# Causal attention: maxima subtracted beside full-array work, row tiles of two batches adjacent, h normalised a step ahead, weights halved on ScalarE

## The chip, the cores and the metric

The program runs on one core of a Trainium2 chip. The metric is device time in microseconds (us), from the start of one execution to its end. The engines of the core work from queues of their own and wait for each other on semaphores: PE (TensorE, matrix multiplication; PEld is its weight load), DVE (VectorE), ACT (ScalarE), POOL (GpSimd) and SP (SyncE, which issues transfers here).

## The reference

The network is a decoder of two layers on x of shape 16 x 128 x 256, each with self attention, cross attention and a gated MLP. Only the first self attention is touched by the change:

```python
x = x + _L0_attn_ref(_layernorm(x, axis=-1), L0_attn_Wqkv, L0_attn_Wout)

def _L0_attn_ref(x, Wqkv, Wout):          # 16 heads of 16, S = 128
    qkv = x @ Wqkv.T                      # split into q, k, v by head
    q = q * cos + rotate_half(q) * sin
    k = k * cos + rotate_half(k) * sin
    scores = jnp.einsum('bhqd,bhkd->bhqk', q, k) * scale
    scores = jnp.where(causal[None, None], -jnp.inf, scores)
    attn = jax.nn.softmax(scores, axis=-1)
    out = jnp.einsum('bhqk,bhkd->bhqd', attn, v)
    return out @ Wout.T
```

The cross attention that follows reads weights that are split into a high and a low half, so that products of fp32r halves add up to the product in fp32. The split is made during the first self attention, one sixteenth in each of its steps.

## The kernel before

The six sublayers run one after the other, each as a block of five programs, one for an engine. The first is `causal_attention`. It takes the 16 batches one at a time (128 tokens are the 128 partitions, 256 features the columns) through a software pipeline that is written out by hand: `batches` calls `step(t, s)` for t from -2 to 17 on each engine, and in step t an engine works on batches t - 2 to t + 2. The order of an engine's work is the order in which its `step` names it; nothing reorders it later.

Heads are worked on in four slots of four. Slot g uses rows 32g to 32g + 31 of TensorE's array, so that scores are made by row tiles (32 x 128 of the array). A batch has two pairs of slots, pair 0 (slots 0 and 1) and pair 1 (slots 2 and 3), and goes this way:

- DVE normalises x into `h` (`dve_normalise`, L144). PE turns h (`turn`, L670), ACT copies it out as hT, PE projects queries and keys (`project_queries_and_keys`, L691). DVE multiplies by the rotary tables (`multiply_by_tables`, L530 and L533) and adds (`add_turned`, L541). PE turns the result (L670 with `weights_even` as its source). ACT copies it out for bf16 (`narrow_queries_and_own_keys`, L452 and L454) and for fp32 (`copy_keys_and_own_queries`, L458 and L460).
- PE computes `scores(b, s, pair)` with bf16 row tiles (L629) only to find a maximum for each row: DVE takes it (`row_maxima`, L549), and POOL spreads it over the columns of the mask (`mask_maxima`, L404, one for a slot).
- PE's `scores_transposed(b, s, pair)` first subtracts these maxima, with the whole array (eight 128 x 128 matmuls in bf16, L643), and adds the fp32 scores on top with row tiles (L651). ACT takes the exponential (`exponentials`, L468).
- PE weighs the values (`weigh_values`, L665, column tiles), ACT copies the result, PE turns it (L732), DVE divides (`normalise_heads`, L556 and L558), PE turns the heads and projects them (`project_heads`, L683), DVE adds to x (`update_x`, L564) and takes the statistics for the next layer.

`lay_mask` (ACT, L476) writes the causal mask into the two banks that the bf16 scores are added to. `chunk_statistics` are the mean and variance of x for four batches at a time, on DVE (L196 to L204) with a power on POOL (L210).

In a step PE's order is: subtract and fp32 scores of pair 0 of batch t; turn h of t + 2, heads of t - 2, queries and keys of t + 1; weigh values of t - 1; project values of t + 1 and heads of t - 2; bf16 scores of pair 0 of t + 1; subtract and fp32 scores of pair 1 of t; project queries and keys of t + 2; turn the output of t - 1; bf16 scores of pair 1 of t + 1.

The split of the cross attention's weights takes three instructions in a step: DVE masks off the low bits (`take_high`, L576, after the maxima of pair 1), POOL subtracts this from the weights for the low half (L412) and the low half from the weights for the high half (L415). In POOL's queue both stand between `mask_maxima` of pair 1 of batch t and `mask_maxima` of pair 0 of batch t + 1. `weights_high` is the semaphore on which L412 waits.

Of the kernel before, what the change touches and what calls it, by code (L numbers as in the profile page):

```python
# [178 lines left out]
CHUNKS = 4  # L179
# [112 lines left out]
def causal_attention(nc, core, dram, weights, next_weights, high_weights, low_weights):  # L292
# [11 lines left out]
    with ExitStack() as ctx:  # L304
# [35 lines left out]
        high_slice = [place(SLICE) for s in range(2)]  # L340
# [15 lines left out]
        weights_high, weights_low, weights_split = sem("weights_high"), sem("weights_low"), sem("weights_split")  # L356
# [3 lines left out]
        def chunk_at_end_of(t):  # L360

            return t + 3 if isinstance(t, int) and t + 3 in range(1, CHUNKS) else None
# [23 lines left out]
        def _(pool):  # L386
# [22 lines left out]
            def split_weights(b, s):  # L409
                part = slice_of(to_split, b)  # L410
                pool.wait_ge(weights_high, b + 1)
                pool.tensor_tensor(slice_of(low_weights, b), part, high_slice[s][:, :], ALU.subtract)\  # L412
                    .then_inc(weights_low, 1)
                pool.wait_ge(weights_low, b + 1)
                pool.tensor_tensor(slice_of(high_weights, b), part, slice_of(low_weights, b).bitcast(F32),  # L415
                                   ALU.subtract).then_inc(weights_split, 1)

            def step(t, s):
                if batch_there(t):
                    mask_maxima(t, s, 1)  # L420
                if batch_there(t):
                    split_weights(t, s)
# [9 lines left out]
        def _(act):  # L432
# [58 lines left out]

            def step(t, s):
# [18 lines left out]
                if batch_there(t + 1):  # L511
                    copy_keys_and_own_queries(t + 1, 1 - s)
                if batch_there(t + 1) and not begins(t + 1):
                    lay_mask(t + 1, 1)
                if batch_there(t):
                    exponentials(t, 1)
# [3 lines left out]
        def _(dve):  # L520
# [51 lines left out]
            def take_high(b, s):  # L572
                if isinstance(b, int) and b == 0:
                    dve.wait_ge(core.weights_loaded[n + 1], 16 * WEIGHT_PARTS)
                dve.wait_ge(weights_low, nonneg(b - 1))
                dve.tensor_scalar(high_slice[s].bitcast(I32), slice_of(to_split, b).bitcast(I32), HIGH_BITS,  # L576
                                  None, ALU.bitwise_and).then_inc(weights_high, 1)

            def step(t, s):
                if batch_there(t + 2):  # L580
                    layer.dve_normalise(dve, t + 2)
                if batch_there(t + 1):
                    add_turned(t + 1)
                if batch_there(t):
                    row_maxima(t, s, 1)
                    take_high(t, s)
# [4 lines left out]
                if batch_there(t - 2) and not left_to_next(t - 2):  # L591
                    statistics(t - 2)
                if batch_there(t + 2):
                    multiply_by_tables(t + 2)
# [5 lines left out]
                if isinstance(t, int) and t == 1:  # L600
                    dve.wait_ge(chunk_statistics.rstd_ready, CHUNKS - 1)
# [3 lines left out]
        def _(pe):  # L605
# [29 lines left out]
            def scores_transposed(b, s, pair):  # L635

                for j in range(2):
# [4 lines left out]
                    for m in range(PER):  # L642
                        pe.matmul(bank_scoresT[j][:, m * P:(m + 1) * P], masked_maxima[g][:, m, :],  # L643
                                  core.minus_ident_bf[:, :], start=(m == 0), stop=False, skip_group_check=True)
                if pair == 0:
# [48 lines left out]
            def step(t, s):  # L694
                if batch_there(t):
                    scores_transposed(t, s, 0)
                if batch_there(t):
                    pe.wait_ge(v_ready, t + 1)
                if batch_there(t + 2):
                    pe.wait_ge(layer.h_ready, t + 3)  # L700
# [16 lines left out]
                if batch_there(t - 2):  # L717
                    if batch_there(t + 1):
                        pe.wait_ge(qk_read, t + 2)
                    project_heads(t - 2)  # L720
                if batch_there(t + 1):
                    scores(t + 1, 1 - s, 0)
# [11 lines left out]
                if batch_there(t + 1):  # L734
                    scores(t + 1, 1 - s, 1)
            batches(pe, step)


# [2451 lines left out]
```

## Time and profile before

| what | value |
|---|---|
| three runs | 1566.97, 1569.88 and 1570.82 us, median 1569.88 us |
| span of the profiled execution, first to last instruction | 1564.6 us (its time with what lies around it is not listed) |
| busy in the span: PE, DVE, ACT, POOL | 95%, 68%, 62%, 46% |
| the causal attention: first h to first h of the cross attention | 8.9 to 202.3 us |

The span is 2.4 to 6.2 us under the listed runs. In the timelines of the profile a row is a run of equal instructions on one engine: its start, how long it took in all, line, operation, what it writes and reads, and how many they are; in brackets, how long the engine was idle before and whose end released it. `weights_even` is a large buffer whose free parts the causal attention uses for many tiles, so that this name alone doesn't tell a tile; the line does. Some fp32 matmuls stand there twice (four of L651 in the order are x8 in a timeline).

### The profile page before, as it was taken

The numbers are of one execution on the slowest core, as the hardware profiler recorded it, in microseconds if no ns is written. First come the engines' busy times: TensorE is split into PE (matmuls) and PEld (weight loads), VectorE is DVE, ScalarE is ACT, GpSimd is POOL, SyncE is SP. The second block draws the span as 40 slices with busy tenths as digits, with TensorE's granted clock in tenths as the row PEclk, the third lists the DMA queues.
The fourth block names the chain that finished last, engine by engine and source line by source line (L and its number), as shares of the span: only waits on it lengthen the run. The fifth ranks groups of instructions, "written<-read, shape, count | busy, mean of one in ns | idle before, by whom it ended". The sixth has DMA issues, their size and how long they took to land. (4 is left out here: it accounts for less than half of the span.)

```text
span 1564.6 us, 30305 instructions
## 1 busy us (share of the span) xinstructions
PE 1485.5 (95%) x10256; PEld 1212.1 (77%) x10256; DVE 1068.3 (68%) x2475; ACT 965.8 (62%) x2612; POOL 727.0 (46%) x891
## 2 busy tenths in 40 slices
PE   5999979999999999899997999899999999989998
PEld 2666668888888888788874555489999999967887
DVE  4676657888888887655545777655566665588887
ACT  2667647777777777533325877577777777742222
POOL 3666625555555555233333433213444444447675
PEclk8999989999999999999997999999999999999999
DMA  6000020000000000000003000020000000000000
GB/s 246 2 1 1 2 97 5 3 5 3 5 3 4 3 3 2 22 1 1 1 5 130 2 2 1 15 92 8 8 8 8 1 8 5 1 1 14 11 15 17
DMA packets 15609, 29.82 MB, mean 19 GB/s; under 512 B 1505, under 2 KB 12002, under 8 KB 14690
## 3 DMA queue, kind: packets, MB, share of 16 engines
q1 hardware_dynamic: 15458, 27.89, 4.9%
q8 instruction: 84, 1.38, 0.4%
q14 instruction: 67, 0.55, 0.1%
HBM read 25.79 MB, written 2.10 MB: 18 GB/s over the span
## 5 line engine op out<-in xcount | busy, mean ns | idle before, releaser
L1453 POOL TENSOR_TENSOR weights_even<-weights_even,cross_reciprocal 128x512 f32<-128x512 f32 x64 | 66.6, 1041 | 201.9 <-DVE cross_reciprocal L1686 201.9
L934 POOL TENSOR_TENSOR cross_work<-cross_work,cross_reciprocal 128x512 f32<-128x512 f32 x64 | 66.6, 1040 | 174.6 <-DVE cross_reciprocal L1091 174.6
L1535 ACT ACTIVATE weights_even<-bank,cross_shift 128x128 f32<-128x128 f32 x256 | 90.5, 366 | 79.1 <-DVE cross_shift L1678 79.1
L1157 PE MATMUL bank<-ident,cross_work 128*128 128x128 f32 x768 | 117.6, 276 | 2.5 <-DVE cross_work L1069 2.2
L987 ACT ACTIVATE cross_work<-bank,cross_shift,cross_q_rms 128x128 f32<-128x128 f32 x256 | 113.6, 455 | 5.2 <-DVE cross_shift L1063 4.0
L1157 PEld LDWEIGHTS bank<-ident,cross_work 128*128 128x128 f32 x768 | 90.2, 141 | 30.0 <-DVE cross_work L1069 21.1
L2481 DVE TENSOR_REDUCE grouped_maxima<-bank 128x4 bf16<-128x512 f32 x128 | 82.3, 684 | 35.9 <-PE bank L2564 35.9
L1962 POOL TENSOR_TENSOR mlp_low_inner<-mlp_inner,mlp_high_inner 128x512 fp32r<-128x512 f32 x36 | 48.7, 1353 | 116.4 <-ACT mlp_high_inner L2005 116.4
L1676 DVE TENSOR_REDUCE cross_maxima<-bank 128x4 f32<-128x512 f32 x64 | 44.1, 690 | 84.6 <-PE bank L1818 84.6
L404 POOL TENSOR_TENSOR causal_masked_maxima<-causal_maxima,causal_constants 128x512 bf16<-128x512 bf16 x64 | 67.0, 1068 | 56.6 <-DVE causal_maxima L549 56.6
L2830 ACT ACTIVATE mx_silu<-bank 128x512 f32<-128x512 f32 x32 | 19.1, 598 | 113.4 <-PE bank L2980 113.3
L1182 PE MATMUL bank<-high_weights,cross_high 128*128 128x512 f32 x192 | 87.0, 453 | 0.0
L1846 PE MATMUL bank<-cross_high_wo,cross_high_heads 128*128 128x256 f32 x256 | 78.5, 306 | 5.8 <-DVE cross_low_heads L1670 5.8
L975 ACT ACTIVATE cross_high_probsT<-bank 128x512 fp32r<-128x512 f32 x64 | 38.4, 599 | 67.7 <-PE bank L1157 67.7
L1800 PE MATMUL bank<-cross_high_hT,late_high 128*128 128x256 f32 x256 | 77.8, 304 | 0.0
L1247 PE MATMUL bank<-cross_high_wo,cross_high_heads 128*128 128x256 f32 x256 | 77.2, 301 | 0.0
L2061 DVE SCALAR_TENSOR_TENSOR mlp_gated<-mlp_tanh,bank 128x512 f32<-128x512 f32 x36 | 24.7, 687 | 76.3 <-ACT mlp_tanh L1999 70.7
L1182 PE MATMUL bank<-high_weights,cross_low 128*128 128x512 f32 x192 | 76.6, 399 | 0.0
L1182 PE MATMUL bank<-low_weights,cross_high 128*128 128x512 f32 x192 | 76.4, 398 | 0.0
L2365 ACT ACTIVATE grouped_probs<-bank 128x512 f32<-128x512 f32 x128 | 68.1, 608 | 10.2 <-PE bank L2597 10.2
L1800 PE MATMUL bank<-cross_low_hT,late_high 128*128 128x256 f32 x256 | 72.2, 282 | 0.0
L1846 PE MATMUL bank<-cross_low_wo,cross_high_heads 128*128 128x256 f32 x256 | 72.2, 282 | 0.0
(375 smaller groups left out, 5292.6 us busy)
## 6 DMA issues: line engine op xcount, KB each, us to landing
weights_even<-in_weights SPq DMA_DIRECT2D x2, 2560.0 KB, 11.8
weights_even<-in_weights SPq DMA_DIRECT2D x2, 1732.0 KB, 8.6
weights_odd_early<-in_weights SPq DMA_DIRECT2D x1, 3072.0 KB, 11.9
weights_odd_values<-in_weights SPq DMA_DIRECT2D x1, 3072.0 KB, 18.9
weights_odd_late<-in_weights SPq DMA_DIRECT2D x2, 1536.0 KB, 9.4
x<-in_x SPq DMA_DIRECT2D x4, 512.0 KB, 8.2
out<-mx_result SPq DMA_DIRECT2D x16, 128.0 KB, 1.7
weights_even<-in_weights SPq DMA_DIRECT2D x2, 512.0 KB, 5.8
```

What stands on the lines that cost most here:

```text
L404: pool.tensor_tensor(masked_maxima[g][:, :, :], maxima[s][:, g, :].unsqueeze(2).to_broadcast([P, PER, P]), later.unsqueeze(1).to_broadcast ...
L934: pool.tensor_tensor(probs[x], probs[x], reciprocal[x][:, :].unsqueeze(2).to_broadcast([P, PER, P]), ALU.mult).then_inc(probs_divided, 1)
L987: last = act.activation(probs[x][:, j, :], bank_scores[:, j * P:(j + 1) * P], ACT.Exp, scale=q_rms[x][:, j:j + 1], bias=shift[x][:, j:j + ...
L1157: last = pe.transpose(bank[:, j * P:(j + 1) * P], source, core.ident[:, :])
L1182: last = pe.matmul(out, half[:, c, :], split_weights[b][:, at:at + PER * D], start=(k == 0), stop=(k == len(jobs) - 1))
L1247: last = pe.matmul(bank_y[:, 0:EMBED], heads[x][a][:, j, :], wo_split[c][:, h, :], start=(g == 0 and m == 0), stop=(g == GROUPS - 1 and m ...
L1453: pool.tensor_tensor(probs[x], probs[x], reciprocal[x][:, :].unsqueeze(2).to_broadcast([P, JOBS, P]), ALU.mult).then_inc(probs_divided, 1)
L1535: last = act.activation(probs[x][:, j, :], bank_scores[x][:, j * P:(j + 1) * P], ACT.Exp, scale=SCALE, bias=shift[x][:, j:j + 1], accum_ou ...
L1800: last = pe.matmul(bank_q[:, j * BOTH * P:(j + 1) * BOTH * P], wqk_split[b][:, c, h * D:(h + 1) * D], hT[s][a][:, c, :, :].rearrange("p b ...
L1846: last = pe.matmul(bank_y[s][:, k * EMBED:(k + 1) * EMBED], heads[x][a][:, k * PER + j, :], wo_split[b][:, g * PER + j, :], start=(g == 0 ...
L2365: act.activation(probs[:, SLOTS * c + j, :], bank_scoresT[j][:, :], ACT.Exp, scale=SCALE)\
L2481: dve.tensor_reduce(maxima[s][:, c, 2 * pair + j, 0:PER], bank_scores[j].rearrange("p (h k) -> p h k", h=PER), AX.X, ALU.max).then_inc(max ...
```

## The change

Four things are changed, all in `causal_attention`:

- On PE the subtraction of the maxima becomes a function of its own, `subtract_maxima`. That of pair 1 of batch t moves ahead of the bf16 scores of pair 0 of t + 1, that of pair 0 of batch t + 1 ahead of the bf16 scores of pair 1 of t + 1. The fp32 scores of pair 0 move from the start of step t to the end of step t - 1, and so stand right behind the bf16 scores of pair 1.
- On DVE `dve_normalise` runs for batch t + 3 at the middle of the step, not for t + 2 at its start; the chunk statistics come one step later.
- On ACT the exponentials of pair 1 come ahead of `lay_mask` of pair 1.
- The high half of the weights is made by a copy on ACT at the end of its step (`take_high`), the low half by one subtraction on POOL (`take_low`); DVE's masking and POOL's second subtraction go. Where `take_low` stands in POOL's step is where the two subtractions stood.

```diff
--- before.py
+++ after.py
@@ -353,13 +352,13 @@
         chunk_statistics = Statistics(layer, "chunk", CHUNK)
         block = ctx.enter_context(nc.Block())
-            return t + 3 if isinstance(t, int) and t + 3 in range(1, CHUNKS) else None
+            return t + 2 if t + 2 in range(1, CHUNKS) else None
 
         def begins(b):
...
@@ -406,20 +405,16 @@
                                            later.unsqueeze(1).to_broadcast([P, PER, P]), ALU.subtract)\
                             .then_inc(maxima_masked, 1)
 
-            def split_weights(b, s):
-                part = slice_of(to_split, b)
+            def take_low(b):
                 pool.wait_ge(weights_high, b + 1)
-                pool.tensor_tensor(slice_of(low_weights, b), part, high_slice[s][:, :], ALU.subtract)\
-                    .then_inc(weights_low, 1)
-                pool.wait_ge(weights_low, b + 1)
-                pool.tensor_tensor(slice_of(high_weights, b), part, slice_of(low_weights, b).bitcast(F32),
-                                   ALU.subtract).then_inc(weights_split, 1)
+                pool.tensor_tensor(slice_of(low_weights, b), slice_of(to_split, b),
+                                   slice_of(high_weights, b).bitcast(F32), ALU.subtract).then_inc(weights_low, 1)
 
             def step(t, s):
                 if batch_there(t):
                     mask_maxima(t, s, 1)
                 if batch_there(t):
-                    split_weights(t, s)
+                    take_low(t)
                 if batch_there(t + 1):
                     mask_maxima(t + 1, 1 - s, 0)
                 if batch_there(t - 2) and not left_to_next(t - 2):
...
+            def take_high(b):
+                if b == 0:
+                    act.wait_ge(core.weights_loaded[n + 1], 16 * WEIGHT_PARTS)
+                act.activation(slice_of(high_weights, b), slice_of(to_split, b), ACT.Copy).then_inc(weights_high, 1)
 
             def step(t, s):
                 if batch_there(t + 2):
...
                 if batch_there(t + 1):
                     copy_keys_and_own_queries(t + 1, 1 - s)
+                if batch_there(t):
+                    exponentials(t, 1)
                 if batch_there(t + 1) and not begins(t + 1):
                     lay_mask(t + 1, 1)
                 if batch_there(t):
-                    exponentials(t, 1)
+                    take_high(t)
             batches(act, step)
 
         @block.vector
...
-            def take_high(b, s):
-                if isinstance(b, int) and b == 0:
-                    dve.wait_ge(core.weights_loaded[n + 1], 16 * WEIGHT_PARTS)
-                dve.wait_ge(weights_low, nonneg(b - 1))
-                dve.tensor_scalar(high_slice[s].bitcast(I32), slice_of(to_split, b).bitcast(I32), HIGH_BITS,
-                                  None, ALU.bitwise_and).then_inc(weights_high, 1)
+            layer.dve_normalise(dve, 0)
 
             def step(t, s):
-                if batch_there(t + 2):
-                    layer.dve_normalise(dve, t + 2)
                 if batch_there(t + 1):
                     add_turned(t + 1)
                 if batch_there(t):
                     row_maxima(t, s, 1)
-                    take_high(t, s)
                 if batch_there(t - 2):
                     update_x(t - 2)
                 if batch_there(t + 1):
                     row_maxima(t + 1, 1 - s, 0)
                 if batch_there(t - 2) and not left_to_next(t - 2):
                     statistics(t - 2)
+                if batch_there(t + 3):
+                    if (t + 3) % CHUNK == 0:
+                        dve.wait_ge(chunk_statistics.rstd_ready, (t + 3) // CHUNK)
+                    layer.dve_normalise(dve, t + 3)
                 if batch_there(t + 2):
                     multiply_by_tables(t + 2)
                 if batch_there(t - 1):
...
@@ -632,7 +628,7 @@
                         if c == EC - 1:
                             last.then_inc(scores_filled, 1)
 
-            def scores_transposed(b, s, pair):
+            def subtract_maxima(b, pair):
 
                 for j in range(2):
                     g = 2 * pair + j
@@ -642,6 +638,9 @@
                     for m in range(PER):
                         pe.matmul(bank_scoresT[j][:, m * P:(m + 1) * P], masked_maxima[g][:, m, :],
                                   core.minus_ident_bf[:, :], start=(m == 0), stop=False, skip_group_check=True)
+
+            def scores_transposed(b, s, pair):
+
                 if pair == 0:
                     pe.wait_ge(q_own_ready, b + 1)
                     pe.wait_ge(k_ready, b + 1)
@@ -692,11 +691,9 @@
                 last.then_inc(qk_filled, 1)
 
             def step(t, s):
-                if batch_there(t):
-                    scores_transposed(t, s, 0)
-                if batch_there(t):
-                    pe.wait_ge(v_ready, t + 1)
                 if batch_there(t + 2):
+                    if batch_there(t):
+                        pe.wait_ge(v_ready, t + 1)
                     pe.wait_ge(layer.h_ready, t + 3)
                     turn(bank_h, layer.h[:, :], layer.hT_filled)
                 if batch_there(t - 2):
...
                     project_heads(t - 2)
+                if batch_there(t):
+                    subtract_maxima(t, 1)
                 if batch_there(t + 1):
                     scores(t + 1, 1 - s, 0)
                 if batch_there(t):
@@ -732,7 +731,9 @@
                         last = pe.transpose(bank_out[:, m * P:(m + 1) * P], outT[:, m, :], core.ident[:, :])
                     last.then_inc(out_turned, 1)
                 if batch_there(t + 1):
+                    subtract_maxima(t + 1, 0)
                     scores(t + 1, 1 - s, 1)
+                    scores_transposed(t + 1, 1 - s, 0)
             batches(pe, step)
 
```

On POOL, from one pair 1 to the next, before (slots are the numbers of `masked_maxima`; `layer_even_31` is `weights_high`):

```order
L404 TENSOR_TENSOR causal_masked_maxima2<-causal_maxima1,causal_constants 128x512 [waits layer_even_22,layer_even_19]
L404 TENSOR_TENSOR causal_masked_maxima3<-causal_maxima1,causal_constants 128x512 [waits layer_even_22,layer_even_19]
L412 TENSOR_TENSOR low_weights<-weights_odd_early,weights_even 128x384 [waits layer_even_31]
L415 TENSOR_TENSOR high_weights<-weights_odd_early,low_weights 128x384 [waits layer_even_32]
L404 TENSOR_TENSOR causal_masked_maxima0<-causal_maxima0,causal_constants 128x512 [waits layer_even_22,layer_even_19]
L404 TENSOR_TENSOR causal_masked_maxima1<-causal_maxima0,causal_constants 128x512 [waits layer_even_22,layer_even_19]
L139 TENSOR_TENSOR rstd<-variance,minus_half 128x1 [waits layer_even_5]
```

and now:

```order
L403 TENSOR_TENSOR causal_masked_maxima2<-causal_maxima0,causal_constants 128x512 [waits layer_even_22,layer_even_19]
L403 TENSOR_TENSOR causal_masked_maxima3<-causal_maxima0,causal_constants 128x512 [waits layer_even_22,layer_even_19]
L410 TENSOR_TENSOR low_weights<-weights_odd_early,high_weights 128x384 [waits layer_even_31]
L403 TENSOR_TENSOR causal_masked_maxima0<-causal_maxima1,causal_constants 128x512 [waits layer_even_22,layer_even_19]
L403 TENSOR_TENSOR causal_masked_maxima1<-causal_maxima1,causal_constants 128x512 [waits layer_even_22,layer_even_19]
L139 TENSOR_TENSOR rstd<-variance,minus_half 128x1 [waits layer_even_5]
```

One subtraction is left between the masks of slot 3 and those of slots 0 and 1, and it waits for the same semaphore, which ACT now raises.

On ACT, the second half of a step and the first row of the next, before (L458 and L460 are the fp32 copies, L476 the mask, L468 the exponentials, L436 hT):

```order
L458 ACTIVATE weights_even<-bank 128x256
L460 ACTIVATE weights_even<-bank,causal_constants 128x2x128 x2
L476 ACTIVATE bank<-causal_constants 128x512 x2
L468 ACTIVATE weights_even<-bank 128x512 x2
L436 ACTIVATE causal_hT<-bank 128x256
```

and now:

```order
L453 ACTIVATE weights_even<-bank 128x256
L455 ACTIVATE weights_even<-bank,causal_constants 128x2x128 x2
L463 ACTIVATE weights_even<-bank 128x512 x2
L471 ACTIVATE bank<-causal_constants 128x512 x2
L490 ACTIVATE high_weights<-weights_odd_early 128x384
L431 ACTIVATE causal_hT<-bank 128x256
```

The exponentials stand ahead of the mask, and the instruction that raises `weights_high` (L490 here) is the last of the step.

On PE, from the projection of heads to the turning of h, before:

```order
L683 MATMUL bank<-weights_even,causal_headsT 128x256 x2
L629 MATMUL bank<-causal_kT_bf,causal_qT_bf 128x256 x4
L643 MATMUL bank<-minus_ident_bf,causal_masked_maxima 128x128 x8
L651 MATMUL bank<-weights_even 128x256 x4
L691 MATMUL bank<-weights_even 128x512 x2
L732 MATMUL bank<-ident,weights_even 128x128 x4
L629 MATMUL bank<-causal_kT_bf,causal_qT_bf 128x256 x4
L643 MATMUL bank<-minus_ident_bf,causal_masked_maxima 128x128 x8
L651 MATMUL bank<-weights_even 128x256 x4
L670 MATMUL bank<-ident,causal_h 128x128 x2
L670 MATMUL bank<-ident,causal_heads 128x128 x2
```

and now:

```order
L682 MATMUL bank<-weights_even,causal_headsT 128x256 x2
L639 MATMUL bank<-minus_ident_bf,causal_masked_maxima 128x128 x8
L625 MATMUL bank<-causal_kT_bf,causal_qT_bf 128x256 x4
L650 MATMUL bank<-weights_even 128x256 x4
L690 MATMUL bank<-weights_even 128x512 x2
L731 MATMUL bank<-ident,weights_even 128x128 x4
L639 MATMUL bank<-minus_ident_bf,causal_masked_maxima 128x128 x8
L625 MATMUL bank<-causal_kT_bf,causal_qT_bf 128x256 x4
L650 MATMUL bank<-weights_even 128x256 x4
L669 MATMUL bank<-ident,causal_h 128x128 x2
L669 MATMUL bank<-ident,causal_heads 128x128 x2
```

The subtractions (L643, now L639) stand ahead of the bf16 scores (L629, now L625), next to work on the whole array, and the fp32 scores (L651, now L650) follow the bf16 scores.

## Rows read from the trace of the kernel before

**Rows 1.** Waits, 52 to 185 us: engine, waiter <- releaser: us, times, longest.

```profile
POOL causal_masked_maxima L404 <- DVE causal_maxima L549: 49.9, 13, 4.3
```

**Rows 2.** Timeline of PE, one step: start, us, instruction, count, idle before.

```profile
104.50 0.41 PE L670 MATMUL bank<-ident,causal_h 128*128 128x128 f32 x2 [0.20 <-DVE causal_h L144]
...
105.01 0.66 PE L670 MATMUL bank<-ident,weights_even 128*128 128x128 f32 x4
...
108.53 0.39 PE L629 MATMUL bank<-causal_kT_bf,causal_qT_bf 32*128 32x256 bf16 x4
108.86 0.62 PE L643 MATMUL bank<-minus_ident_bf,causal_masked_maxima 128*128 128x128 bf16 x8
109.41 1.13 PE L651 MATMUL bank<-weights_even 32*128 32x256 f32 x8
110.47 1.98 PE L691 MATMUL bank<-weights_even 128*128 128x512 f32 x4
112.29 0.60 PE L732 MATMUL bank<-ident,weights_even 128*128 128x128 f32 x4
```

**Rows 3.** Timeline of ACT, the same step.

```profile
105.75 0.84 ACT L452 ACTIVATE causal_kT_bf<-bank,causal_constants 128x256 bf16<-128x256 f32 x2
...
107.78 1.09 ACT L468 ACTIVATE weights_even<-bank 128x512 f32<-128x512 f32 x2
...
110.45 1.19 ACT L476 ACTIVATE bank<-causal_constants 128x512 f32<-128x512 f32 x2
111.49 1.15 ACT L468 ACTIVATE weights_even<-bank 128x512 f32<-128x512 f32 x2
```

**Rows 4.** Timeline of POOL, the same step.

```profile
107.75 0.99 POOL L412 TENSOR_TENSOR low_weights<-weights_odd_early,weights_even 128x384 fp32r<-128x384 f32 x1
108.81 1.00 POOL L415 TENSOR_TENSOR high_weights<-weights_odd_early,low_weights 128x384 fp32r<-128x384 f32 x1
109.80 2.04 POOL L404 TENSOR_TENSOR causal_masked_maxima<-causal_maxima,causal_constants 128x512 bf16<-128x512 bf16 x2
```

**Rows 5.** Timeline of DVE, end of the same step.

```profile
114.48 0.40 DVE L144 TENSOR_SCALAR causal_h<-x,mean,rstd 128x256 f32<-128x256 f32 x1
114.80 0.68 DVE L541 TENSOR_TENSOR weights_even<-weights_even 128x512 f32<-128x512 f32 x1
```

**Rows 6.** Timeline of ACT, cross attention: a 128x384 copy to fp32r.

```profile
208.30 0.49 ACT L969 ACTIVATE cross_high<-bank 128x384 fp32r<-128x384 f32 x1
```

**Rows 7.** Timeline of PE in grouped attention: row tiles of two types.

```profile
907.35 0.73 PE L2590 MATMUL bank<-grouped_shifts,ones_bf 32*128 32x512 bf16 x4
907.71 1.23 PE L2597 MATMUL bank<-grouped_q_own,grouped_kT 32*128 32x512 f32 x8
```

**Rows 8.** Busy time by stretch: PE, PEld, DVE, ACT, POOL, then PEclk, DMA share, GB/s.

```profile
63.00:104.80 41.80, 40.98 (x384) 26.80 (x384) 28.98 (x76) 29.92 (x72) 26.50 (x28) 1.00 0.01 2
41.00:44.00 3.00, 3.00 (x34) 2.30 (x38) 2.35 (x4) 1.71 (x5) 2.59 (x3) 0.50 0.00 0
185.00:187.00 2.00, 1.68 (x18) 1.08 (x20) 1.79 (x4) 1.05 (x3) 1.36 (x3) 1.00 0.01 4
188.00:190.00 2.00, 2.00 (x34) 1.41 (x33) 0.00 (x0) 0.38 (x1) 1.92 (x3) 0.50 0.00 0
```

**Rows 9.** Timeline of PE, steps 0 and 1 (early in the stage).

```profile
40.96 0.66 PE L670 MATMUL bank<-ident,causal_h 128*128 128x128 f32 x2 [1.55 <-DVE causal_h L144]
41.47 1.12 PE L670 MATMUL bank<-ident,weights_even 128*128 128x128 f32 x4
```

**Rows 10.** Timeline of PE, steps 14 and 15 (late in the stage).

```profile
178.42 0.66 PE L670 MATMUL bank<-ident,weights_even 128*128 128x128 f32 x4
...
187.50 0.69 PE L670 MATMUL bank<-ident,causal_heads 128*128 128x128 f32 x2
```

**Rows 11.** Timeline of DVE, start of the stage.

```profile
15.56 1.39 DVE L196 BATCH_NORM_STATS2 causal_chunk_stats<-x 128x6 f32<-128x256 f32 x4
...
17.87 0.68 DVE L541 TENSOR_TENSOR weights_even<-weights_even 128x512 f32<-128x512 f32 x1
```

More of the change, by code:

```diff
@@ L339, in causal_attention @@
         to_split = core.region[n + 1]
-        high_slice = [place(SLICE) for s in range(2)]
         bank_scores, bank_scoresT, bank_out = core.banks[0:2], core.banks[2:4], core.banks[4]
@@ L355, in causal_attention @@
         headsT_filled, headsT_ready = sem("headsT_filled"), sem("headsT_ready")
-        weights_high, weights_low, weights_split = sem("weights_high"), sem("weights_low"), sem("weights_split")
+        weights_high, weights_low = sem("weights_high"), sem("weights_low")
         chunk_statistics = Statistics(layer, "chunk", CHUNK)
@@ L599, in step @@
                     chunk_statistics.dve(dve, CHUNK * chunk_at_end_of(t), chunk_at_end_of(t))
-                if isinstance(t, int) and t == 1:
-                    dve.wait_ge(chunk_statistics.rstd_ready, CHUNKS - 1)
             batches(dve, step)
```

## The prediction

> **What bounds the kernel now.** I read the waits of the stage first, then the timelines of one steady step on each engine. From 52 to 185 us POOL's only listed wait is for DVE's maxima, 49.9 us in 13 steps [rows 1], so POOL has 3.8 us to spare in a step; PE has next to none: its only gap in the step is 0.20 us before h [rows 2], and its granted clock is 1.00, the 2.4 GHz level, from 63 to 104.8 us with PE busy 40.98 of 41.80 us [rows 8]. So the stage is PE's own sum, and a step takes 10.53 us: the turn of queries and keys of step 1 starts at 41.47, that of step 14 at 178.42 [rows 9, 10], and 136.95 / 13 = 10.53. I call the start of this turn Q (105.01 in the step shown [rows 2]) and count times in a step from it.
>
> **What the change takes from PE.** A pair's bf16 scores, subtraction and fp32 scores take 0.33 + 0.55 + 1.06 = 1.94 us, from 108.53 to 110.47 [rows 2], and row tiles and full array alternate. Now the two row-tile groups adjoin and lie on different rows of the array. Grouped attention shows such a pair: the bf16 tiles at 907.35 last 0.73 us, yet the fp32 tiles start at 907.71, 0.36 us later, and run beside them [rows 7]. So the fp32 scores should start when the bf16 ones are half issued. My estimate is 0.13 us for the bf16 slot (bounds 0.1 and the old 0.33), 0.95 for the fp32 slot (1.06 less a first weight load that now lies beside the bf16 tiles; bounds 0.95 and 1.06), and 0.1 us less for the subtraction, which follows full-array work without a switch: 0.4 us a pair (bounds 0 and 0.45), 0.8 a step. I take the upper part, because the row with two types is the nearest. h, a step ahead, ends the 0.20 us gap. DVE loses its masking and POOL one subtraction of 1.00 us [rows 4]; both engines had time there, so this alone is worth nothing.
>
> **The wait that the change adds.** `take_low` is in POOL's queue behind the masks of pair 1 of batch t and ahead of those of pair 0 of t + 1. Today it finds its input ready: the two subtractions start at 107.75 and 108.81, back to back with the masks at 109.80 [rows 4]. Now the input is ScalarE's copy, the last instruction of ScalarE's step. When is it done? ScalarE starts on the turned queries and keys at Q + 0.74 and reaches what was the mask of pair 1 at 110.45, Q + 5.44 [rows 3]. There the exponentials of pair 1 stand now. Their scores come in time: PE's subtraction of the second slot waits for the exponentials of pair 0, which end at 107.78 + 1.09, Q + 3.86, with 0.06 us to hand over, and half a subtraction slot with its switch (0.32), 0.13 and 0.95 follow, so they are there at Q + 5.4. Exponentials, then mask, 1.04 us each by start to start (110.45 to 111.49), then the copy, 0.49 as another copy of this shape to fp32r [rows 6] (bounds 0.4 and 0.6): the high half is ready at 5.44 + 1.04 + 1.04 + 0.49 = Q + 8.01. POOL was free for it at 107.75, Q + 2.74. So POOL stands 5.3 us, with the masks of pair 0 of t + 1 queued behind, whose maxima are long there.
>
> PE waits for these masks. It reaches the subtraction for pair 0 of t + 1 at about Q + 5.3 (projection of queries and keys) + 1.82 + 0.53 (to the end of the output's turn, 110.47 to 112.29 and on [rows 2]) = Q + 7.65. The masks are ready at 8.01 + 0.1 (two hand-overs) + 1.06 + 1.02 = Q + 10.2 for slot 0 and Q + 11.2 for slot 1 [rows 4]. PE idles 2.5 us, works 0.2, and idles 0.8. Behind the subtraction in PE's queue stand the bf16 scores of pair 1, the fp32 scores that ScalarE's next exponentials need, and the turns of h, heads, queries and keys: everything that lets ScalarE reach its next copy. So this is a loop, and its length is the step:
>
> 8.01 to the copy + 0.1 + 1.06 for the low half + 2.04 for two masks + 0.05 to PE + 0.32 + 0.13 + 0.95 on PE + 0.51 for h and heads (104.50 to 105.01 [rows 2]) = 13.2 us.
>
> The 0.8 us saved on PE lies half inside this loop, and is in it; without the overlap of row tiles it would be 13.2 + 0.6 = 13.8. That the two normalisations and the chunk statistics moved costs nothing here: DVE is done with the next queries and keys well before PE's wait ends.
>
> **The clock.** After gaps PE's clock falls in this stage: PE had waited 1.55 us for h [rows 9], and from 41 to 44 us the clock is 0.50, the 1.2 GHz level; PE busy 1.68 of 2.00 us from 185 to 187 us is followed by 0.50 from 188 to 190 [rows 8]. Every step would now hold 3.3 us of idle within 3.5. At 0.50 the turn of queries and keys takes 1.12 us against 0.66 [rows 9, 2], 1.7 times. If the low clock covers PE's piece of the loop after the wait, 0.32 + 0.13 + 0.95 + 0.51 = 1.91 us, it adds 0.7 x 1.91 = 1.3; a part that reaches past Q adds some 0.3 more, since PE there has only 0.2 us of slack against ScalarE. I take 1.6: a step of 14.8 us. Ends: 0 (no fall, 13.2), and the low clock for the whole step, where PE's three pieces of the loop cost 1.3 + (1.7 x 3.65 - 3.92 = 2.3) + 0.7 x 1.45 = 4.6 more (17.8). I take the value near the first, because a low stretch here was followed by full clock while PE was kept busy.
>
> The Trainium skill says in "TensorE: Matmul & The Clock Gate", section "A second HAM failure mode: psum-queue depth-cycling", that short idles between groups of matmuls can make the clock swing between its two levels, at a cost in throughput. By that each step pays as in the 14.8; if it didn't hold the sum would be that of 13.2. The rows above side with it.
>
> **The sum.** 13 steps from Q of step 1 to Q of step 14: 13 x 14.8 - 136.95 = +55.4. From there to the turn of heads of step 15: before 187.50 - 178.42 = 9.08 [rows 10]; now 8.01 + 0.1 + 1.06 + 2.04 + 0.05 + 1.40 = 12.7, and 1.3 for the clock: +4.9. Start: chunk statistics and normalisation leave the place ahead of the first `add_turned`, 17.87 - 15.56 = 2.3 us earlier [rows 11]; the first such wait, between steps 0 and 1, takes about as much back: 0, give or take 2. Ends of the stage: -0.4 for the switches. Together +60 on this execution's span of 1564.6; what lies around it is taken as it was, so the median of 1569.9 becomes **1630 us**. With a step of 14.2 or 15.4 it is 1622 or 1638.
>
> **Rivals.**
> 1. The wait is there and the clock holds. 13 x 13.2 - 136.95 = +34.7, +3.6 at step 14, -2 at the start: 1606 us. For it: PE still works three quarters of each step. Against: the two falls in rows 8 after less idle.
> 2. The clock stays low through most of the stage: 13 x 17.8 - 136.95 = +94.5, +6: 1670 us. For it: each wait may come before the clock has risen. Against: 10 us of unbroken PE work lie between waits.
> 3. The other side, faster: POOL's masks don't wait behind `take_low`. Then ScalarE's exponentials of pair 0 and DVE's chain would set the step: Q to the projection 3.86 + 0.06 + 0.32 + 0.13 + 0.95 = 5.3, from the projection to the end of `add_turned` 114.48 (the place of h, which leaves [rows 5]) + 0.68 + 0.06 - 110.47 = 4.75: 10.05 us. 13 x (10.53 - 10.05) = 6.2 us; 2.3 won at the start, 2.0 lost to the third chunk, now in a step that has no slack: 1563 us. It decides where the copy is done 3.1 us before PE needs the masks, by Q + 4.5; the order has it at Q + 8, and on POOL the low half stands first. No row here shows POOL waiting with ready work behind.
> 4. The row tiles don't overlap although the rest is as forecast: 13 x 0.6: 1638, inside the range.
>
> The Trainium skill bears on the third: "TensorE: Matmul & The Clock Gate", section "Architectural detail: the array is 16× 32×32, not 1× 128×128", says that GpSimd takes its queue strictly in order. By it the third rival falls and 1630 stands, without it 1563 could come.
>
> **How the numbers follow.** A run of this kernel tells some 0.3%, 4.7 us, from no change. Forecast, 1618 to 1645, with rival 4: 0.67. Clock holds, about 1606: 0.17. Clock low throughout: 0.08. POOL not held, about 1563: 0.05. The rest, near no change: 0.03. The range takes the first two and their neighbours, 1602 to 1652. Faster 0.05, same 0.03, slower 0.92.
>
> **What would show it.** In the trace after, POOL's mask rows at the low half's line should wait for ScalarE's copy, some 5 us in each step, where they waited for DVE; PE's subtraction should have 2.5 us and 0.8 us of idle put down to the masks; the turn of queries and keys should come every 14 to 15.5 us; PEclk should show 0.5 in parts of each step; the fp32 scores should start about 0.13 us behind the bf16 ones. A step near 10 us, or a copy that ends ahead of Q + 4.5, would make the forecast wrong; a step of 13.2 with PEclk at 1.00 would leave the wait right and the clock wrong.

## The result and the profile after

The changed kernel takes 1635.67 us (median of 4 runs, 1633.14 to 1642.64) against 1568.43 (4 runs, 1560.91 to 1570.82): a ratio of 1.045, with a 95% interval of 1.0419 to 1.0481. The forecast was slower, 1630 us, between 1602 and 1652. The profiled execution has a span of 1634.8 us, 70.2 more than before.

The waits from 40 to 260 us (engine, waiter <- releaser: us, times, longest) show what stands in the place of [rows 1]:

```profile
POOL low_weights L410 <- ACT high_weights L490: 117.6, 14, 9.2
...
PE bank L639 <- POOL causal_masked_maxima L403: 50.4, 28, 4.2
```

POOL waits at the low half for ScalarE's copy, and PE waits for the masks that stand behind it. The turn of queries and keys (Q in the prediction, now L669) of step 1 and of step 14, in PE's timeline, against [rows 9, 10]:

```profile
39.22 1.06 PE L669 MATMUL bank<-ident,weights_even 128*128 128x128 f32 x4
...
243.28 1.06 PE L669 MATMUL bank<-ident,weights_even 128*128 128x128 f32 x4
```

These 13 steps take 204.06 us where they took 136.95: 15.70 a step on average against 10.53, +67.1 in all. Q of step 1 comes 2.25 us earlier than before (41.47 - 39.22). One step on PE, from Q to Q (start, us, instruction, count, in brackets idle before and its releaser), answers [rows 2]:

```profile
133.68 1.06 PE L669 MATMUL bank<-ident,weights_even 128*128 128x128 f32 x4
...
137.81 0.61 PE L639 MATMUL bank<-minus_ident_bf,causal_masked_maxima 128*128 128x128 bf16 x8
138.36 0.28 PE L625 MATMUL bank<-causal_kT_bf,causal_qT_bf 32*128 32x256 bf16 x2
138.37 0.48 PE L650 MATMUL bank<-weights_even 32*128 32x256 f32 x2
138.48 0.27 PE L625 MATMUL bank<-causal_kT_bf,causal_qT_bf 32*128 32x256 bf16 x2
138.69 0.81 PE L650 MATMUL bank<-weights_even 32*128 32x256 f32 x6
139.43 1.98 PE L690 MATMUL bank<-weights_even 128*128 128x512 f32 x4
...
144.35 0.38 PE L639 MATMUL bank<-minus_ident_bf,causal_masked_maxima 128*128 128x128 bf16 x4 [2.50 <-POOL causal_masked_maxima L403]
145.80 0.58 PE L639 MATMUL bank<-minus_ident_bf,causal_masked_maxima 128*128 128x128 bf16 x4 [1.06 <-POOL causal_masked_maxima L403]
...
149.24 1.06 PE L669 MATMUL bank<-ident,weights_even 128*128 128x128 f32 x4
```

This step takes 149.24 - 133.68 = 15.56 us; most of the others take 15.74 to 15.83. PE idles 2.50 us, works, and idles 1.06. What it waits for stands in the timelines of ACT, POOL and DVE of the same step, against [rows 3 to 5]:

```profile
139.59 1.10 ACT L463 ACTIVATE weights_even<-bank 128x512 f32<-128x512 f32 x2
140.56 1.14 ACT L471 ACTIVATE bank<-causal_constants 128x512 f32<-128x512 f32 x2
141.60 0.54 ACT L490 ACTIVATE high_weights<-weights_odd_early 128x384 fp32r<-128x384 f32 x1
...
132.57 2.04 POOL L403 TENSOR_TENSOR causal_masked_maxima<-causal_maxima,causal_constants 128x512 bf16<-128x512 bf16 x2 [1.23 <-DVE causal_maxima L551]
142.21 0.99 POOL L410 TENSOR_TENSOR low_weights<-weights_odd_early,high_weights 128x384 fp32r<-128x384 f32 x1 [7.60 <-ACT high_weights L490]
143.17 2.48 POOL L403 TENSOR_TENSOR causal_masked_maxima<-causal_maxima,causal_constants 128x512 bf16<-128x512 bf16 x2
...
138.85 1.29 DVE L551 TENSOR_REDUCE causal_maxima<-bank 128x4 bf16<-128x512 f32 x2 [0.41 <-PE bank L625]
...
143.41 1.34 DVE L543 TENSOR_TENSOR weights_even<-weights_even 128x512 f32<-128x512 f32 x1
```

The copy ends at 142.14, Q + 8.46, the low half starts 0.07 us later, and the masks follow, although their maxima were there at 140.14 (138.85 + 1.29). The pair of masks takes 2.48 us where it took 2.04, and DVE's sum, which starts among them, 1.34 where it took 0.68 [rows 4, 5]. The busy time by stretch (PE, PEld, DVE, ACT, POOL, then PEclk, DMA share, GB/s) of this step's pieces and of the stage answers [rows 8]:

```profile
132.00:135.00 3.00, 3.00 (x22) 2.01 (x22) 1.09 (x2) 0.83 (x3) 2.04 (x2) 0.50 0.02 5
135.50:145.50 10.00, 6.74 (x63) 4.36 (x52) 6.17 (x16) 6.64 (x16) 3.29 (x3) 1.00 0.00 0
145.70:149.20 3.50, 3.40 (x20) 2.41 (x21) 1.29 (x2) 0.00 (x0) 1.86 (x3) 0.50 0.00 0
53.90:243.00 189.10, 146.50 (x1155) 101.11 (x1154) 88.95 (x215) 97.26 (x228) 71.84 (x73) 0.82 0.00 1
```

In every step the clock falls to the 1.2 GHz level (0.50) behind the idle and comes back to 2.4 GHz (1.00) while PE is kept busy: 0.82 over the stage. Q takes 1.06 us in all 14 steps, against 0.66 in [rows 2].

### The profile page after: what moved, and what is told of

It reads as the page before. It is cut to its first block and busy times, and to the rows that moved or that the text cites. A ratio compares the mean times of both kernels' runs of the same rounds, so it can differ in the third digit from the quotient of the medians.

```text
span 1634.8 us, 30297 instructions
## 1 busy us (share of the span) xinstructions
PE 1508.4 (92%) x10256; PEld 1233.9 (75%) x10256; DVE 1067.6 (65%) x2459; ACT 975.3 (60%) x2628; POOL 715.6 (44%) x875
## 5 line engine op out<-in xcount | busy, mean ns | idle before, releaser
L403 POOL TENSOR_TENSOR causal_masked_maxima<-causal_maxima,causal_constants 128x512 bf16<-128x512 bf16 x64 | 70.6, 1124 | 25.9 <-DVE causal_maxima L551 24.6
L639 PE MATMUL bank<-minus_ident_bf,causal_masked_maxima 128*128 128x128 bf16 x256 | 23.9, 228 | 54.7 <-POOL causal_masked_maxima L403 53.7
L551 DVE TENSOR_REDUCE causal_maxima<-bank 128x4 bf16<-128x512 f32 x64 | 41.2, 686 | 48.1 <-PE bank L625 48.1
## 6 DMA issues: line engine op xcount, KB each, us to landing
weights_odd_late<-in_weights SPq DMA_DIRECT2D x2, 1536.0 KB, 10.4
```

The costliest lines, as they stand in the source:

```text
L403: pool.tensor_tensor(masked_maxima[g][:, :, :], maxima[s][:, g, :].unsqueeze(2).to_broadcast([P, PER, P]), later.unsqueeze(1).to_broadcast ...
```

## The experiments

Ratios are against the kernel before in the same set of runs (1565.74 to 1567.08 us); a step is the usual distance of two Qs in the steady part. By this measure a step of the changed kernel is 15.78 us; the 15.70 above is the average over 13 steps, with some shorter ones among them.

**Is it the low half's place on POOL?** `low_last` is the changed kernel with `take_low` behind the masks:

```diff
                     mask_maxima(t, s, 1)
-                if batch_there(t):
-                    take_low(t)
                 if batch_there(t + 1):
                     mask_maxima(t + 1, 1 - s, 0)
+                if batch_there(t):
+                    take_low(t)
```

> The changed kernel with one move: on POOL the subtraction for the low half stands last in the step, behind the masks of pair 0 of the next batch. Theory (POOL's wait for ScalarE's copy holds the masks, and with them PE): PE's idle before the subtraction goes, PEclk is 1.00 in the stage, the step falls from 15.7 to about 10.05 us, and the time from 1636 to about 1559 (1555 to 1564), so below the kernel before. Rival (the new order of PE's work, row tiles beside each other, or ScalarE's longer step costs the time): a step of 13 us or more, over 1600 us.

Measured: 1562.31 us, ratio 0.9977 (0.9958 to 0.9996), step 10.24. POOL's and PE's timelines:

```profile
106.60 2.04 POOL L403 TENSOR_TENSOR causal_masked_maxima<-causal_maxima,causal_constants 128x512 bf16<-128x512 bf16 x2 [2.85 <-DVE causal_maxima L551]
109.21 0.99 POOL L410 TENSOR_TENSOR low_weights<-weights_odd_early,high_weights 128x384 fp32r<-128x384 f32 x1 [0.57 <-ACT high_weights L490]
...
111.32 0.66 PE L669 MATMUL bank<-ident,weights_even 128*128 128x128 f32 x4 [0.16 <-DVE weights_even L543]
```

The low half still waits for the copy, 0.57 us, but nothing that PE needs stands behind it, and the slowdown is gone: 15.78 - 10.24 = 5.5 us a step hang on this one place. PE now waits 0.16 us for DVE's sum ahead of Q.

**Or is it when the copy is done?** `copy_first` leaves POOL's order and puts the copy at the start of ScalarE's step:

```diff
+                if batch_there(t):
+                    take_high(t)
...
                     exponentials(t, 1)
-                if batch_there(t):
-                    take_high(t)
```

> The changed kernel with ScalarE's halving at the start of its step, ahead of the exponentials; GpSimd's order stays, take_low ahead of the masks. Theory (only the time at which the halving is done decides, and where it is done by Q+4.5 GpSimd isn't held, as the prediction's third rival has it): GpSimd's wait of take_low for the halving falls from 8.9 us to under 1 us, the wait for the masks ahead of the subtraction is gone, step 10.0 to 10.4 us, 1558 to 1566 us. Rival (take_low's place ahead of the masks is what costs, wherever the halving stands): a step above 11.5 us and over 1580 us.

Measured: 1565.93 us, ratio 1.0001 (0.9983 to 1.0019), step 10.24. POOL's timeline of a step, and ScalarE's of the first copy:

```profile
107.48 0.99 POOL L410 TENSOR_TENSOR low_weights<-weights_odd_early,high_weights 128x384 fp32r<-128x384 f32 x1
110.37 2.04 POOL L403 TENSOR_TENSOR causal_masked_maxima<-causal_maxima,causal_constants 128x512 bf16<-128x512 bf16 x2 [1.90 <-DVE causal_maxima L551]
...
28.79 0.52 ACT L490 ACTIVATE high_weights<-weights_odd_early 128x384 fp32r<-128x384 f32 x1 [8.55 <-DMA weights_odd_values<-in_weights]
```

The low half ahead of the masks costs nothing once its input is there. So it takes both, the place on POOL and the late copy; mending either gives the same step. What `copy_first` loses against `low_last` lies at the start: its Q of step 1 comes at 41.20, that of `low_last` at 37.40, and the 13 steps behind it take the same time. There its first copy waits 8.55 us for the weights, at the head of ScalarE's queue.

**Does PE's new order matter for the slowdown?** `halving_alone` is the kernel before with the halving alone (the `take_high` and `take_low` pieces of the change's diff; ScalarE's exponentials of pair 1 stay behind the mask, and DVE keeps its old order); `old_pe_order` is `low_last` with PE's order of before.

> The kernel before with the halving of the changed one alone: ScalarE's copy last in its step, POOL's one subtraction where the two stood; PE's and DVE's orders as before. Theory: the same loop through ScalarE, POOL and PE, a step of 15.5 to 16.2 us, 1635 to 1645 us, at least as slow as the changed kernel. Rival (the slowdown needs the new order on PE): a step of 10.5 to 11 us, 1568 to 1576 us.

Measured: 1637.66 us, ratio 1.0451 (1.0427 to 1.0476), step 15.34. The halving is enough. POOL's timeline, and DVE's sum:

```profile
110.27 1.00 POOL L410 TENSOR_TENSOR low_weights<-weights_odd_early,high_weights 128x384 fp32r<-128x384 f32 x1 [8.25 <-ACT high_weights L490]
111.22 2.08 POOL L403 TENSOR_TENSOR causal_masked_maxima<-causal_maxima,causal_constants 128x512 bf16<-128x512 bf16 x2
...
112.33 1.52 DVE L543 TENSOR_TENSOR weights_even<-weights_even 128x512 f32<-128x512 f32 x1
```

> low_last with PE's order of the kernel before (subtractions and fp32 scores where they stood); h a step ahead, halving and POOL's order as in low_last. In low_last PE saves 0.43 us a pair, but stands again before the second subtraction of pair 1 (ScalarE's exponentials) and before the turn of queries and keys (DVE's sum). Theory (the saving of the row tiles goes into these two waits): here both waits are gone or short, the step is 10.3 to 10.4 us against 10.24, the time 1563 to 1566. Rival (the row tiles side by side are what makes low_last faster): a step of 10.5 or more, 1568 to 1573 us.

Measured: 1562.58 us, ratio 0.9986 (0.9968 to 1.0004), step 10.19 against 10.24, a little shorter than the 10.3 to 10.4 expected. In this run PE is busy for 100.00 of the 100.00 us from 62 to 162, so PE's own sum is the step. In `low_last` it is busy for 97.62 of them: there the row tiles' saving on PE goes into waits and comes to nothing.

**What does the clock cost?** `gap_filled` gives PE 16 matmuls more in a step, 12 and 4 ahead of the two waits for the masks, into banks that the subtraction then starts anew:

```diff
                     pe.wait_ge(probs_ready, nonneg(i - 1))
+                    if pair == 0 and b > 1:
+                        for k in range((12, 4)[j]):
+                            pe.matmul(bank_scoresT[j][:, :], core.ident_bf[:, :],
+                                      mask_qk[:, :].unsqueeze(1).to_broadcast([P, PER, P]), start=True, stop=True)
                     pe.wait_ge(maxima_masked, i + 1)
```

> The changed kernel with 16 matmuls a step added on PE in the gap (12 of 128x512 in bf16 while PE would wait for the first mask, 4 before the second), into banks that the subtraction overwrites; the result is not changed by them. Theory (the low clock adds about 2 us to a step, on top of the wait): PEclk 1.00 from step 2 on, the wait for POOL stays, the step falls from 15.7 to about 13.6 us, the time to 1604 to 1612. Rival (the clock's share is small, the loop itself is 15.7 us at either clock): 1630 to 1640 us; if the added work itself delays PE it is slower still.

Measured: 1606.36 us, ratio 1.0262 (1.0234 to 1.0289), step 13.52. Busy time over the stage:

```profile
53.90:227.00 173.10, 168.27 (x1425) 101.52 (x1427) 93.89 (x228) 100.07 (x241) 75.87 (x77) 1.00 0.01 1
```

More work on PE makes the kernel 29 us faster than the changed one: the clock stays at 1.00, and 15.78 - 13.52 = 2.26 us a step were its price.

**What does DVE's sum cost beside the masks?** `sum_after_masks` holds the sum back until both masks are made:

```diff
                 dve.wait_ge(qk_read, b + 1)
+                if 2 <= b:
+                    dve.wait_ge(maxima_masked, SLOTS * (b - 1) + 2)
                 dve.wait_ge(qkT_filled, nonneg(b))
```

> The changed kernel with one wait more: DVE's sum of the two rotary products starts only when POOL has made both masks of pair 0. In the changed kernel the sum takes 1.32 us beside the masks and 0.68 alone in the kernel before, and the pair of masks 2.48 against 2.04. Theory (the two engines slow each other): the sum is back at 0.68, the pair of masks at 2.04, the step 0.4 us shorter, the time 5 to 7 us lower, 1629 to 1631. Rival (the masks are slow for another reason, or the later sum becomes the wait): 1636 us or more.

Measured: 1628.17 us, ratio 1.0382 (1.0355 to 1.0408), step 15.01. POOL's and DVE's timelines:

```profile
109.27 2.04 POOL L403 TENSOR_TENSOR causal_masked_maxima<-causal_maxima,causal_constants 128x512 bf16<-128x512 bf16 x2
...
111.40 0.69 DVE L545 TENSOR_TENSOR weights_even<-weights_even 128x512 f32<-128x512 f32 x1 [1.78 <-POOL causal_masked_maxima L403]
```

Apart, they take 2.04 and 0.69 us again; a wait added to DVE shortens the step by 15.78 - 15.01 = 0.77, about twice the 0.4 expected.

**Is that all?** `filled_and_apart` makes both edits.

> gap_filled and sum_after_masks in one: sixteen matmuls more a step keep the matrix engine busy while it waits for the masks, and the vector engine adds the sum only once both masked maxima are there. gap_filled alone left a step of 13.52 us at a granted clock of 1.00; sum_after_masks alone took some 0.7 us off a step at the lower clock. Theory (what stands between the 15.7 us of the changed kernel and the 13.2 us worked out is the clock and the contention of the two engines, and nothing else): step 12.9 to 13.2 us, clock 1.00 from step 2 on, the masks at 2.04 us each, 1598 to 1602 us. Rival (at full clock the sum is late in place of the masks, as Q waits for it): step 13.4 to 13.6 us, 1604 to 1608 us, no gain over gap_filled.

Measured: 1595.48 us (4 runs), ratio 1.0195 (1.0172 to 1.0219), step 13.17: Q to Q in PE's timeline with the second subtraction, ScalarE's copy of that step, and the stage's busy time:

```profile
104.33 0.60 PE L675 MATMUL bank<-ident,weights_even 128*128 128x128 f32 x4
...
115.62 0.39 PE L645 MATMUL bank<-minus_ident_bf,causal_masked_maxima 128*128 128x128 bf16 x4
...
117.50 0.60 PE L675 MATMUL bank<-ident,weights_even 128*128 128x128 f32 x4
...
111.84 0.56 ACT L490 ACTIVATE high_weights<-weights_odd_early 128x384 fp32r<-128x384 f32 x1
...
51.50:222.70 171.20, 168.56 (x1458) 104.28 (x1460) 86.95 (x229) 102.14 (x247) 71.94 (x79) 1.00 0.01 2
```

The step is the 13.2 that the prediction summed, and the rival (no gain over 13.52) falls. The time is 2.5 us under the range expected and 10.9 under `gap_filled`, while 13 steps of 0.35 make 4.6. The rest lies between executions: the four of `filled_and_apart` had a granted clock of 0.989 to 0.992, those of `gap_filled` 0.980 to 0.990, with times from 1600.80 to 1612.27. At a like clock (0.989 and 0.990) the two kernels take 1598.02 and 1600.80.

**Can the change be made to pay?** Three edits on top of `low_last`, each upon the one before. `h_in_idle` moves `dve_normalise` for t + 3 to right behind the maxima of pair 1:

> low_last with h for batch t + 3 made right after the maxima of pair 1, where DVE is idle 2.5 us, not after the statistics, where it took 0.71 us beside POOL's masks and held DVE's first product by 0.2 us. Theory (DVE's chain to the turn of queries and keys sets the step): the turn comes 0.15 to 0.2 us sooner after the projection, step 10.05 to 10.1, the time 2 to 3 us under low_last, about 1560. Rival (another wait sets the step): 10.24 and 1562 as there.

Measured: 1559.56 us, ratio 0.9973 (0.9958 to 0.9987), step 10.07. `exp_first` puts ScalarE's exponentials of pair 0 ahead of the mask of pair 0:

> h_in_idle with ScalarE's exponentials of pair 0 ahead of its mask for pair 0, so that PE's second subtraction of pair 1 doesn't wait for them (0.27 us in low_last). Theory: step 9.75 to 9.85 us, 5 to 6 us under low_last, about 1557. Rival (the mask, now later, holds the bf16 scores instead): 10.0 us or more, 1560.

Measured: 1557.53 us, ratio 0.9956 (0.9939 to 0.9973), step 9.87, just over the range. `out_first` puts the output's turn ahead of the projection of queries and keys on PE, and the heads' division ahead of the products with the tables on DVE:

> exp_first with the turn of the output ahead of the projection of queries and keys on PE, and DVE's division of the heads ahead of the rotary products, so that it lies beside the projection. Theory (DVE's chain from the projection to the sum is the last wait): the chain is 0.6 us shorter, PE has no wait left, step 9.4 to 9.55 us, the time 1551 to 1554. Rival (the output comes too late from ScalarE, or POOL's masks become last): 9.8 us or more, 1557 us or more.

Measured: 1555.99 us (12 runs), ratio 0.995 (0.9934 to 0.9965), step 9.79: the fastest here, 0.5% under the kernel before, but a miss against 9.4 to 9.55. PE's and DVE's timelines, and last DVE's products in `exp_first`, tell where it stuck:

```profile
106.94 1.88 PE L690 MATMUL bank<-weights_even 128*128 128x512 f32 x4
...
111.12 0.66 PE L669 MATMUL bank<-ident,weights_even 128*128 128x128 f32 x4 [0.18 <-DVE weights_even L543]
...
105.85 1.29 DVE L551 TENSOR_REDUCE causal_maxima<-bank 128x4 bf16<-128x512 f32 x2 [0.48 <-PE bank L625]
...
108.93 0.69 DVE L532 TENSOR_TENSOR weights_even<-bank,causal_constants 128x512 f32<-128x512 f32 x1
...
110.32 0.74 DVE L543 TENSOR_TENSOR weights_even<-weights_even 128x512 f32<-128x512 f32 x1
...
108.28 0.69 DVE L532 TENSOR_TENSOR weights_even<-bank,causal_constants 128x512 f32<-128x512 f32 x1 [0.51 <-PE bank L690]
```

From the products to Q the way is 0.44 us shorter (111.12 - 108.93 = 2.19 against 110.91 - 108.28 = 2.63 in `exp_first`), but from Q to the products it is 0.36 longer (7.60 against 7.24), since the projection now stands behind the output's turn. The projection ends at 106.94 + 1.88 = 108.82, 0.11 us ahead of the products. DVE has no listed idle from the maxima at 105.85 to the end of the sum at 111.06, and its division ends at 108.81, so an earlier projection alone would win little.

## Why the prediction was right

The mechanism is the one forecast, and the place and the late copy were each shown to be needed. The size of the step was not: 15.70 us lies above the 14.8 forecast and above the 14 to 15.5 that was to show it. Its terms, in the prediction's order:

- **PE's saving a pair.** Forecast 0.4 us (0.13 + 0.95 and 0.1 off the subtraction). The pair at 137.81 takes 139.43 - 137.81 = 1.62 against 1.94: 0.32 saved. The split was wrong: the fp32 tiles start 0.01 us behind the first bf16 tiles, keep their 1.06, and the subtraction its 0.55. What the saving is worth in the loop, 0.6 by the forecast, no run takes by itself: `halving_alone` (15.34) and `sum_after_masks` (15.01, masks at 2.08 and 2.04) lie 0.33 apart, but differ in ScalarE's and DVE's order too. With the loop gone it is nothing (`old_pe_order`).
- **POOL's wait.** Forecast 5.3 us; 7.60 in the step shown, 117.6 / 14 = 8.4 on average. POOL was taken to be free at Q + 2.74, but the masks of pair 1 end at 132.57 + 2.04, Q + 0.93. The loop is no longer for that, since the copy ends later in either case.
- **The copy.** Forecast at Q + 8.01; in the step shown Q + 8.46. ScalarE's three pieces are as forecast (0.97 + 1.04 + 0.54 from 139.59); what came later is their start, since the clock is still at 0.50 when Q starts. The prediction had this as 0.3 inside the clock's term.
- **The masks.** Forecast 0.1 + 1.06 + 2.04 + 0.05 = 3.25 from the copy's end to PE's second subtraction; measured 145.80 - 142.14 = 3.66. This is the step that failed: "the two normalisations ... moved costs nothing here: DVE is done ... well before PE's wait ends". DVE had the time, but its sum came to lie beside POOL's masks, which are on the loop. It starts 0.24 us into the first mask (143.41 - 143.17) and the pair takes 2.48. With DVE's old order, the normalisation of h ahead of the sum (`halving_alone`), it starts 1.11 us behind the first mask's start (112.33 - 111.22): there the sum takes 1.52 and the masks only 2.08. The price is 0.35 us a step at full clock (13.52 - 13.17) and 0.77 with the falling clock (15.78 - 15.01).
- **The loop by hand.** Forecast 13.2, measured 13.17 once clock and contention are taken away (`filled_and_apart`). Its three parts fit too: the copy ends at Q + 8.07 (111.84 + 0.56 - 104.33; forecast 8.01), the second subtraction starts 115.62 - 112.40 = 3.22 later (3.25), and Q comes 117.50 - 115.62 = 1.88 behind it (1.91).
- **The clock.** Forecast 1.6; without the contention it is 15.01 - 13.17 = 1.84, with it 2.26. PE's piece from the second subtraction to Q takes 149.24 - 145.80 = 3.44, where 1.91 + 1.3 were forecast. What the prediction cites from the Trainium skill ("TensorE: Matmul & The Clock Gate", "A second HAM failure mode: psum-queue depth-cycling"), that short idles can make the clock swing at a cost, agrees with this trace: 0.50, 1.00, 0.50 within one step.
- **The sum.** In the step shown 0.15 (copy: 0.45, less the 0.3 already counted) + 0.41 (masks) + 0.23 (PE) on 14.8 make 15.6; measured 15.56. On average the step was 0.9 us short (15.70 against 14.8): about a third of it is the contention, the rest the clock (2.26 for 1.6 by the experiments). Over 13 steps that is +67.1 for +55.4. From Q of step 14 to the turn of heads of step 15 it is 258.91 - 243.28 = 15.63, +6.55 for +4.9. Against that, the start won 2.25 where 0 was taken. The span grew by 70.2 us where 60 was forecast, the median by 67.2. That the time still lies within 6 us of 1630 is in part luck: the start's gain, and a median before that came out 1.45 us lower with a fourth run (1568.43 for 1569.88).
- **Rivals.** Rival 1 (clock holds) is what `gap_filled` and `filled_and_apart` make by force; by itself the clock fell. Rival 2 fell: the clock is 1.00 for the 10 us from 135.5 to 145.5 of the step shown. Rival 3 is `low_last` and `copy_first`; in the changed kernel POOL stood idle at the low half until 142.21 with the maxima of the next masks there since 140.14: it took its queue in order, as the prediction cites from the Trainium skill ("TensorE: Matmul & The Clock Gate", "Architectural detail: the array is 16× 32×32, not 1× 128×128"). The rival's step of 10.05 came as 10.24, since the normalisation of h lay beside POOL's masks there. Moved away in `h_in_idle`, the step is 10.07. Rival 4 fell with the pair at 1.62.

That normalisation in `low_last`, by DVE's timeline, took 0.71 us where it takes 0.40 in [rows 5], while POOL's masks ran from 106.60 to 108.64:

```profile
108.08 0.71 DVE L144 TENSOR_SCALAR causal_h<-x,mean,rstd 128x256 f32<-128x256 f32 x1
```

## What to carry to other kernels

Work that is off the critical path costs nothing only if nothing that is on it stands behind it in a queue: before a wait is put into an in-order queue, look up when its input is ready and what is next in that queue. Here a wait in a loop that PE closes was paid once in idle and a second time in clock; filling the idle with useless matmuls was a cheap way to measure the second part. Where two engines' instructions come to lie beside each other for the first time, their durations from the old trace are to be taken as a lower bound, and which of the two starts first is to be looked up.

## What the runs showed of the hardware

- **DVE and POOL hold each other up.** The sum on DVE reads two operands in SBUF, as do POOL's masks: 0.68 to 1.34 us and 2.04 to 2.48 us side by side, 0.69 and 2.04 apart. The Trainium skill says in "SBUF — State Buffer", section "Who interferes with whom", that a DVE instruction with two SBUF inputs contends with a GpSimd instruction that reads SBUF, and that the order of issue decides who blocks. The trace agrees: the sum, begun 0.24 us into the first mask, took 0.66 longer and that mask did not (1.04 us), while the second mask, begun beside the sum, took 1.49, 0.45 longer. In `halving_alone` the sum began when the second mask had started, and paid alone: 1.52, with both masks at 2.08.
- **Row tiles of other rows start early.** The fp32 tiles at 138.37 start ahead of the second bf16 tiles at 138.48, which stand ahead of them in PE's order. For these starts it doesn't hold that nothing reorders an engine's work, as the description of the kernel before has it.
- **More PE work, less time.** 16 added matmuls a step took 29 us off the kernel, by a clock of 1.00 in place of 0.82.
